# Order of two blocks of matmuls in a linear attention kernel: the product of state and queries behind the product of masked scores and values

## The reference

```python
qkv = silu(xn @ qkv_w.T)                      # q, k, v of each head, 128 columns
# over blocks of 32 tokens, per head and batch entry:
intra = ((cq @ ck.T) * diag_decay) @ cv
inter = (cq * q_decay) @ kv
kv    = kv * block_decay + (ck * k_decay).T @ cv
attn  = intra + inter
# then an RMS norm over all heads, times norm_w, times sigmoid(xn @ gate_w.T), @ out_w.T
```

## The kernel before

| step | TensorE | ScalarE | VectorE |
|---|---|---|---|
| 1 | prod(QK1, 3), inter, attend, prod(QK2, 1), scores(2) | silu(QK1, "r"), squares(1), ..., keys(2), ..., probs(2) | fade_cross(1), add_cross(1), gate_att(1), mask(2) |
| 2 | prod(QK2, 7), inter, attend, prod(QK2, 4), scores(3), prod(QK2, 3), prod(G23, 1), state(3) | squares(2), hi(QK2, "p"), silu(QK2, "q"), gated_hi(2), silu, hi, hi, probs(3), keys(3) | make_c22(QK2), fade_cross(2), add_cross(2), gate_att(2), lo(QK2, "p"), mask(3) |
| 3 | output(1), inter, attend, prod(G23, 7), output(2), prod(G23, 5), output(3) | weight(QK3, 4), hi(QK2, "r"), squares(3), keys(4) | add_out(1), lo(QK2, "r"), fade_cross(3), add_cross(3), gate_att(3), add_out(2) |
| 4 | scores(5), inter, attend, prod(QK3, 3, 4), state(5), prod(QK0, 1), output(6), inter(5), attend(5) | hi(QK3, "p"), probs(5), keys(5), squares(4), state_high(5), silu, hi, gated_hi(4) | mask(5), lo(QK3, "p"), fade_cross(4), add_cross(4), gate_att(4), probs_lo(5), make_c12, state_low(5), gated_lo(4) |
| 6 | prod(QK0, 7), inter, attend, prod(QK0, 4), scores(7), prod(QK0, 3), state(7), prod(G01, 1), output(8), inter(7) | hi(QK0, "p"), squares(6), silu, keys(7), gated_hi(6), hi, probs(7), state_high(7) | lo(QK0, "p"), fade_cross(6), add_cross(6), gate_att(6), mask(7), gated_lo(6), lo, probs_lo(7), make_c12, state_low(7) |

## Time and profile before

### The profile page before, as it was taken

How to read it: one execution, slowest core, us unless ns; L and a number is a source line. 1 busy time by engine, 2 the same in 40 slices (tenths; PEclk the granted TensorE clock), 3 DMA queues, 4 the chain that set the end, 5 groups by cost and what they waited for, 6 DMA issues and landing times.

```text
span 1067.5 us, 20381 instructions
## 1 busy us (share of the span) xinstructions
PE 1057.5 (99%) x6290; PEld 937.9 (88%) x6290; DVE 644.8 (60%) x1196; ACT 678.7 (64%) x1465; POOL 633.1 (59%) x626
## 2 busy tenths in 40 slices
PE   8999999999999999999999999999999999999997
PEld 7998889888898889988899888988889888998897
DVE  6866564656546575565746656465655647456566
ACT  9677565766567575675757656576666757567631
POOL 5558573674737646475645846376474755548554
PEclk9999999999999999999999999999999999999998
DMA  8223222131213222122211312223130322123232
GB/s 302 84 56 92 57 65 60 54 86 45 62 54 97 68 62 59 44 79 59 64 55 54 89 39 61 59 68 91 38 89 14 105 59 64 56 59 89 65 105 80
DMA packets 124579, 77.10 MB, mean 72 GB/s; under 512 B 82784, under 2 KB 104544, under 8 KB 124512
## 3 DMA queue, kind: packets, MB, share of 16 engines
q1 hardware_dynamic: 124224, 75.84, 24.9%
q10 hardware_dynamic: 288, 0.52, 0.1%
HBM read 63.23 MB, written 13.11 MB: 72 GB/s over the span
## 4 chain that ended last, share of the span: by engine, by line
PE 95%; DVE 1%; POOL 1%; DMA 1%; issue 1%; ACT 1%; SPq 0%; DVEq 0%; ACTq 0%; POOLq 0%
PE bank_q L1932 8%; PE bank_q L1933 8%; PE bank_q L1934 8%; PE bank_r L1932 6%; PE bank_p L1933 6%; PE bank_p L1934 6%; PE bank_p L1932 6%; PE bank_r L1933 6%; PE bank_r L1934 6%; PE outp L1932 5%; PE outp L1933 5%; PE outp L1934 5%; PE att L2037 4%; PE side L2018 3%; PE score L1992 3%; PE att L2043 3%
## 5 line engine op out<-in xcount | busy, mean ns | idle before, releaser
L475 POOL TENSOR_TENSOR w_lo<-combo,w_hi 128x768 fp32r<-128x768 f32 (+1 forms) x128 | 165.0, 1297 | 121.6 <-ACT w_hi L671 121.5
L475 POOL TENSOR_TENSOR w_lo<-raw,w_hi 128x256 fp32r<-128x256 f32 (+1 forms) x128 | 131.3, 1029 | 84.7 <-ACT w_hi L671 83.5
L526 POOL TENSOR_TENSOR sum_sq<-sum_sq,square 128x512 f32<-128x512 f32 x64 | 82.8, 1293 | 100.2 <-ACT square L849 100.2
L1500 DVE TENSOR_TENSOR acc<-acc,outp 128x512 f32<-128x512 f32 x116 | 79.1, 682 | 63.9 <-PE outp L1934 63.9
L1932 PE MATMUL bank_q<-c_hi,w_hi 128*128 128x512 f32 x276 | 108.5, 393 | 0.0
L1933 PE MATMUL bank_q<-c_lo,w_hi 128*128 128x512 f32 x276 | 107.9, 391 | 0.0
L1934 PE MATMUL bank_q<-c_hi,w_lo 128*128 128x512 f32 x276 | 107.8, 391 | 0.0
L1932 PE MATMUL outp<-wo_hi,g_hi 128*128 128x512 f32 x250 | 98.3, 393 | 0.2
L1933 PE MATMUL outp<-wo_lo,g_hi 128*128 128x512 f32 x250 | 97.9, 392 | 0.0
L1934 PE MATMUL outp<-wo_hi,g_lo 128*128 128x512 f32 x250 | 97.5, 390 | 0.0
L671 ACT ACTIVATE w_hi<-combo 128x768 fp32r<-128x768 f32 (+1 forms) x128 | 81.0, 634 | 21.1 <-issue 11.2
(11 more groups left out here) (321 smaller groups left out, 3467.7 us busy)
## 6 DMA issues: line engine op xcount, KB each, us to landing
raw<-w_chunks SPq DMA_DIRECT2D x165, 256.0 KB, 3.3
keys_dram<-cross SPq DMA_DIRECT2D x192, 32.0 KB, 1.6
keys_t<-keys_dram SPq DMA_DIRECT2D x96, 64.0 KB, 2.4
near_dram<-near SPq DMA_DIRECT2D x2, 2048.0 KB, 9.7
table<-near_dram SPq DMA_DIRECT2D x32, 128.0 KB, 2.0
fade<-near_dram SPq DMA_DIRECT2D x32, 128.0 KB, 2.9
y<-x SPq DMA_DIRECT2D x8, 256.0 KB, 2.9
out<-acc SPq DMA_DIRECT2D x7, 256.0 KB, 2.1
```

Source lines behind the costliest of these rows:

```text
L475: pool.tensor_tensor(piece(w_lo[i % 2], j), piece_source(i, j), piece(w_hi[i % 2], j).bitcast(F32), ALU.subtract).then_inc(wlo[j], 1)
L526: pool.tensor_tensor(sum_sq[:, s % 2, :], sum_sq[:, s % 2, :], square[:], ALU.add).then_inc(summed, 1)
L1500: dve.tensor_tensor(tile, tile, outp, ALU.add).then_inc(acc_done, 1)
```

## The change

In steps 0, 1, 2, 3, 4 and 6 of each group, `attend(s)` is issued ahead of `inter(s)` instead of behind it, on TensorE alone. Steps 5 and 7 stay. No instruction is added or removed, no wait is changed, and the other engines' lists are the same. The diff makes the same six swaps in the list of the last group and in that of the others:

```diff
                 prod(V2, 5, 4, 3)
+                attend(0)
                 inter(0)
-                attend(0)
                 prod(QK1, 1, 6)
...
                 prod(QK1, 3)
+                attend(1)
                 inter(1)
-                attend(1)
                 prod(QK2, 1)
...
                 prod(QK2, 7)
+                attend(2)
                 inter(2)
-                attend(2)
                 prod(QK2, 4)
...
                 output(1)
+                attend(3)
                 inter(3)
-                attend(3)
                 prod(G23, 7)
...
                 scores(5)
+                attend(4)
                 inter(4)
-                attend(4)
                 prod(QK3, 3, 4)
...
                 prod(QK0, 5, 7)
+                attend(6)
                 inter(6)
-                attend(6)
                 prod(QK0, 4)
```

## The result

The changed kernel takes **1079.36 us** (median of 6 runs, 1077.43 to 1080.18) where the kernel before takes 1069.74 in the same series (6 runs, 1068.47 to 1070.13). The ratio is 1.009, with a 95% interval of 1.0077 to 1.0103: slower, as forecast, and 2 us above the 1077.4 of the forecast. The medians differ by 9.6 us where the forecast has 8.1. The profiled execution, the shortest of the six, has an own time of 1077.43 and a span of 1075.6.

What follows compares the result with a forecast made beforehand. TensorE, busy for 99% of the span, was taken to bound the kernel. Terms of 1.6 + 4.3 - 1.6 + 3.8 = +8.1 us on a profiled 1069.3 gave 1077.4 us, range 1072 to 1083.5.

Steps and rivals of the forecast that it cites:

- Steps 0 and 1: First two steps of a group: fade_cross comes late anyway or VectorE's idle time before mask(2) absorbs the delay; 0.
- Step 2: Later fade_cross delays ScalarE through keys(3), so state(3) on TensorE starts +0.20 later; eight groups, +1.6 us.
- Step 3: Later q_hi delays VectorE's add_out(2), so output(3) waits 0.45 plus 0.09 restart; 0.54 in eight groups, +4.3 us.
- A: Start time of the swapped inter and attend pair on TensorE, from which the forecast counts later starts.
- Step 4: Earlier att lets mask(5) and its chain start earlier, so attend(5) waits less; -0.20 in eight groups, -1.6 us.
- Step 6: Later q_hi delays keys(7) and state_low(7), so state(7) and inter(7) wait; 0.54 in seven groups, +3.8 us.
- Faster: Only the earlier att_ready reaches TensorE, with output(3), state(3), state(7) covered; -1.6 to -2, 1067.5 us; chance 0.04.
- Part: ScalarE and VectorE close up in steps 2 and 6; only steps 3 and 4 count: +2.7, 1072.0 us; chance 0.08.
- No change: Both orders alike for readers, since VectorE comes late to both in steps 0, 3, 4, 6; 1069.3 us; chance 0.03.
- Clock: New waits in each group bring a stretch of 6.6 us at 1.2 instead of 2.4 GHz; 1104 us; chance 0.01.

Runs made afterwards that it cites:

- The last experiment: Changed kernel, all six swaps kept, with add_out(2) ahead of gate_att(3), keys(3) of probs(3), keys(7) of silu(QK0, "q"): 1070.95 us, ratio 1.0017.
- the second: Second trace, from running the unaltered changed kernel once more in another series: 1078.57 us, ratio 1.0077 to the kernel before.
- the eight waits: Changed kernel plus eight waits on a semaphore long reached, at the head of ScalarE's loop body: 1079.51 us, ratio 1.0095.

## Why the prediction was right

**That a swap costs TensorE nothing by itself:** right. inter and attend take 1.51 together in the new order (482.65 to 484.16) and 1.52 in the old. att was whole 0.36 earlier, as mask(5)'s idle time shows.

**Steps 0 and 1, 0:** right; no jump in either trace, and no cost when swapped alone.

**Step 2, +0.20 in each group:** right, 0.22. The back-to-back chain through ScalarE to keys(3) passed the delay on whole. The low bound of the range assumed that it would give some of it up.

**Step 3, +0.54:** right in mechanism, and undersized in six groups of eight. In the first and last group it is 0.45 + 0.08 = 0.53. In the others it is 0.62 + 0.11. The step that failed is "How soon ScalarE follows that signal is shown in step 4: ... so 0.10": here it was 0.38. q_hi moved from A+0.90 to A+2.05, by 1.15 and not 0.88. VectorE made up 0.12 of it on the way, since add_out(2) moved from A+4.47 to A+5.50. That is 1.2 us over the whole kernel, the largest miss of any term. Of the stated bounds, 3.5 to 6.4 for this step, it stays inside.

**Step 4, -0.20:** right in seven groups, -0.17 on average, and -1.15 when swapped alone. In the last group the jump changes from one execution to the next and is no effect of the swap that could be counted on.

**Step 6, +0.54 in seven groups:** the size is right, 3.9 against 3.8, and so is its split. The two parts are one delay, and the forecast reckoned with that: it asks whether inter(7) could start at 528.00 "where the shifted TensorE wants it at 527.99", so the 0.34 lost at state(7) is taken off there. Without this 0.34 the same working gives 0.35 of wait for the fourth group, with a restart 0.45. The last experiment measured 0.48. It was the expectation of that experiment that forgot this and let inter(7) keep its 1.2 us.

**The sum:** +8.1 forecast, +8.2 in the first trace and +9.8 in the second. The places that the forecast priced add up to 9.7 and 10.0, close to the 9.6 between the medians and 1.6 above the forecast. In the first trace 0.75 of this came back in the tail, 0.27 at output(10), and the rest in small jumps. The window of 6.6 us around the wait for sum_sq, laid as in the earlier trace rows, 1.2 us ahead of the first matmul behind it, with the granted clock third from the end:

```profile
1053.90:1060.50 6.60, 5.39 (x27) 5.02 (x28) 5.17 (x11) 0.50 (x1) 2.61 (x2) 0.74 0.21 79
```

The mean was 0.74, in the kernel before 0.50, so the low clock lasted a shorter time. That the profiled execution met the forecast to 0.1 us is luck: none of this was in the forecast, and the median is 2 us above it. One sign was read wrong beforehand: TensorE's busy time was to stay near 1057 and is 1061.1, for the reason given above with its rows.

**The rivals.** Faster: the wait that speaks for it is not in the loop, as the prediction has it, but in the last group, and the view shows none of the shorter ones at attend(5) of the loop. Its reason, the gain at attend(5), is real; its condition, cover at output(3), state(3) and state(7), was absent in all three. Part: ScalarE and VectorE closed up by 0.12 in step 3 and hardly at all in steps 2 and 6. No change: refuted by q_hi, which had no wait ahead of it before and holds the chain now. Clock: the granted clock stayed at its upper level, 2.4 GHz, through the new waits:

```profile
484.00:496.00 12.00, 11.54 (x52) 9.25 (x51) 5.72 (x10) 6.94 (x13) 7.95 (x10) 1.00 0.20 55
```

The rule of the Trainium skill that spoke for this rival (TensorE: Matmul & The Clock Gate, "A second HAM failure mode: psum-queue depth-cycling") is not borne out here: three to four waits of 0.1 to 0.7 us in each group of 125 us did not lower the clock.

**Left open:** whether the transfer of instructions is what delays q_hi; why one group in eight loses 0.4 at inter(7), and not always the same; and why the tail's wait for GpSimd varies from 2.7 to 4.3 us between kernels.

## What to carry to other kernels

When two blocks of an engine without slack are swapped, their own time is not the question. List who waits for each result, move those starts by the exact distance, and follow each strict queue to the next instruction that the full engine needs; here four matmuls, 6 to 9 us behind their swaps, carried the cost. An instruction that empties a buffer and stands behind unrelated waits, as add_out(2) did, is the first to move ahead. Before it is priced as saved, look whether the same late chain meets the full engine again at its next need.

## What was not expected of the hardware

A q_hi that waited for inter started 0.10 us after the modelled end of its last matmul, and 0.37 to 0.39 at one place, step 3 of each of the six loop groups. This was so in all six traces with the swap of step 3 and without the eight waits; the eight waits brought it to 0.10. A packet of instructions starts just behind this q_hi in each of these groups. The Trainium skill (Perfetto Trace Analysis, "DVE / Act Engine Instruction") has fetch and decode ahead of the wait for the signal, so a late fetch would look like this; the packets fit it, and no run here shows that it is one. In the kernel before, the packet starts at the same q_hi, but this one never waited for its signal, so no delay shows. Where ScalarE's loop turns, the same queue is seen at work, and ScalarE stands idle for 1.7 to 2.5 us each time.
